# Two of eight one-hot comparisons per half chunk move from VectorE to GpSimd

## The reference, cut to what matters

```python
w = lut[idx]                               # lut: 16 numbers, idx: int32
return jnp.einsum('bsh,oh->bso', x, w)
```

## Time and profile before

| | |
|---|---|
| median of three runs | 1895.86 us (1895.57 to 1897.36) |
| profiled execution, span from first to last instruction | 1894.3 us |
| that execution's own device time | not given beside the span; the span is 1.6 us under the median |
| front block | from 0 to about 526 us of the span |
| VectorE busy, whole span | 1313.4 us (69%) |
| GpSimd busy, whole span | 791.7 us (42%) |
| mean granted TensorE clock | 0.890 |

### The profile page before, as it was taken

One profiled execution on the slowest core, in us unless ns is written; L12 is line 12 of the kernel. 1 busy time (PEld: TensorE's weight loads), 2 busy tenths in 40 slices (PEclk: granted clock), 3 DMA queues, 4 the chain that ended last, 5 costly groups with the idle time before them and its releaser, 6 DMA issues. The chain is left out here.

```text
span 1894.3 us, 26370 instructions
## 1 busy us (share of the span) xinstructions
PE 1535.1 (81%) x9320; PEld 1312.2 (69%) x9328; DVE 1313.4 (69%) x1918; ACT 910.7 (48%) x1579; POOL 791.7 (42%) x477
## 2 busy tenths in 40 slices
PE   5857778676528986996898799648899999999896
PEld 3445355444427986895897689637779899998785
DVE  6677597776559989999998999624445555555452
ACT  3444546445224445344444534414456666666563
POOL 1010000010045456445654643357735666762555
PEclk9879788897758997997998799858999999999998
DMA  7988799985572582375359236459998999999876
GB/s 210 344 282 273 280 323 369 332 266 176 165 311 77 191 345 76 124 278 223 106 190 372 73 119 236 165 189 342 388 365 235 253 260 259 256 261 220 228 168 78
DMA packets 187942, 445.47 MB, mean 235 GB/s; under 512 B 41616, under 2 KB 43664, under 8 KB 177568
## 3 DMA queue, kind: packets, MB, share of 16 engines
q1 hardware_dynamic: 115040, 283.37, 44.3%
q0 software_dynamic: 31760, 74.48, 16.8%
q10 hardware_dynamic: 41008, 85.89, 12.5%
HBM read 246.77 MB, written 205.28 MB: 239 GB/s over the span
## 5 line engine op out<-in xcount | busy, mean ns | idle before, releaser
L1429 POOL TENSOR_TENSOR mix_st<-mix_Bb,mix_du 128x2048 f32<-128x2048 f32 x64 | 293.4, 4584 | 267.9 <-DVE mix_st L2149 255.1
L2141 DVE TENSOR_TENSOR_SCAN mix_st<-mix_YY,mix_st 128x512 f32<-128x512 f32 x256 | 311.8, 1218 | 53.7 <-POOL mix_st L1429 32.2
L1847 ACT ACTIVATE mix_YY<-mix_dt,mix_A 128x512 f32<-128x512 f32 x256 | 176.9, 691 | 277.6 <-DVE mix_st L2141 273.6
L1473 POOL DMA_INDIRECT out_x<-moe_ys,moe_meta x130 | 209.6, 1613 | 192.4 <-ACT moe_ys L1973 93.5
L1594 PE MATMUL mix_G<-mix_xThi,mix_wup 128*128 128x256 f32 x1408 | 272.4, 290 | 15.2 <-issue 14.5
L1594 PEld LDWEIGHTS mix_G<-mix_xThi,mix_wup 128*128 128x128 f32 x1408 | 231.3, 199 | 18.1 <-issue 16.7
L1755 PE MATMUL mix_Dp<-moe_xhi,moe_whi 128*128 128x288 f32 x768 | 233.2, 304 | 1.1 <-DVE moe_wlo L2245 1.1
L1755 PE MATMUL mix_Dp<-moe_xhi,moe_wlo 128*128 128x288 f32 x768 | 227.5, 296 | 0.0
L1755 PE MATMUL mix_Dp<-moe_xlo,moe_whi 128*128 128x288 f32 x768 | 227.4, 296 | 0.0
L1620 PE MATMUL mix_YY<-mix_ident,mix_st 128*128 128x128 f32 x1024 | 145.2, 297 | 95.4 <-DVE mix_st L2149 95.2
L2255 DVE TENSOR_TENSOR moe_xlo<-mix_G,moe_xhi 128x512 fp32r<-128x512 f32 (+1 forms) x160 | 102.0, 638 | 163.1 <-ACT moe_xhi L1936 160.4
(11 more groups left out here) (216 smaller groups left out, 3059.5 us busy)
## 6 DMA issues: line engine op xcount, KB each, us to landing
x_by_expert<-front_zeros ACTq DMA_DIRECT2D x16, 4480.0 KB, 23.9
mix_wup<-w_halves SPq DMA_DIRECT2D x44, 1024.0 KB, 5.6
moe_raw<-in_ew SPq DMA_DIRECT2D x32, 1280.0 KB, 8.4
moe_xt<-x_by_expert SPq DMA_DIRECT2D x128, 256.0 KB, 8.4
mix_wdn<-w_halves SPq DMA_DIRECT2D x44, 512.0 KB, 6.5
front_idx<-in_idx SPq DMA_DIRECT2D x44, 384.0 KB, 9.1
w_halves<-front_wst SPq DMA_DIRECT2D x44, 384.0 KB, 7.8
mix_Bb<-bc_rows SPq DMA_DIRECT2D x16, 1024.0 KB, 9.9
```

Source lines behind the costliest of these rows:

```text
L1429: nc.gpsimd.tensor_tensor(st[:, g % STBUF, :, :], Bb[:, q, :, :], du[:, k % 2, :].unsqueeze(1).to_broadcast([P, NG, S]), ALU.mult).then_in ...
L1473: pool.indirect_dma_start(out=out_rows, out_offset=bass.IndirectOffsetOnAxis(ap=meta[0:rows, e % MBUF, j, 0:1].bitcast(U32), axis=0), in_= ...
L1847: nc.scalar.activation(dA, dt[:, k % 2, :], ACT.Exp, scale=A[:, c, m:m + 1]).then_inc(da_ready, 1)
L2141: nc.vector.tensor_tensor_scan(r, dA, r, 0.0, ALU.mult, ALU.add).then_inc(scanned, 1)
```

## The change

Of each half's eight one-hots GpSimd makes j = 2 and j = 6 and VectorE the other six. GpSimd runs the same comparison on the same operands, counted on a semaphore of its own; `lookup(t)` and `load_idx(h)` wait for whichever engine made the one-hot. `kcol` is signalled to GpSimd. GpSimd's one-hots stand in its list `AHEAD` = 4 slots ahead as well, the first two on either side of `scale_and_shift(0)`, and behind the other work of each slot.

```diff
+ON_POOL = (2, 6)
+def onehots(t, pool):
+    n = sum(1 for j in ON_POOL if j < t % PAIRS)
+    return len(ON_POOL) * (t // PAIRS) + n if pool else t - (len(ON_POOL) * (t // PAIRS) + n)
...
             def load_idx(h):
-                    sp.wait_ge(onehot_made, PAIRS * (h - 1))
+                    sp.wait_ge(onehot_made, onehots(PAIRS * (h - 1), False))
+                    sp.wait_ge(pool_onehot_made, onehots(PAIRS * (h - 1), True))
...
         def _(pool):
+            def one_hot(t):
+                h, j = divmod(t, PAIRS)
+                if t >= SLOTS or j not in ON_POOL:
+                    return
+                if j == ON_POOL[0]:
+                    pool.wait_ge(idx_in[h % 2], 32 * (h // 2) + 32)
+                if t >= OH:
+                    pool.wait_ge(slot_done, t - OH + 1)
+                nc.gpsimd.tensor_scalar(oh[:, t % OH, :], idx[:, h % 2, :], kcol[:, j:j + 1], None,
+                                        ALU.is_equal).then_inc(pool_onehot_made, 1)
+            pool.wait_ge(pool_kcol, 1)
+            for t in range(AHEAD - 2):
+                one_hot(t)
             scale_and_shift(0)
+            for t in range(AHEAD - 2, AHEAD):
+                one_hot(t)
             for t in range(SLOTS + 16):
...
+                one_hot(t + AHEAD)
...
             def lookup(t):
-                pe.wait_ge(onehot_made, t + 1)
+                if j in ON_POOL:
+                    pe.wait_ge(pool_onehot_made, onehots(t + 1, True))
+                else:
+                    pe.wait_ge(onehot_made, onehots(t + 1, False))
...
         def _(dve):
             def one_hot(t):
+                if j in ON_POOL:
+                    return
...
-            link(nc.vector.tensor_scalar(kcol[ROWS_H:P, :], kcol[ROWS_H:P, :], 1.0, None, ALU.add))
+            nc.vector.tensor_scalar(kcol[ROWS_H:P, :], kcol[ROWS_H:P, :], 1.0, None, ALU.add).then_inc(pool_kcol, 1)
+            dve.wait_ge(pool_kcol, 1)
```

More of the change, by code:

```diff
@@ L233, in front_block @@
         onehot_made = sem("onehot_made")
+        pool_onehot_made = sem("pool_onehot_made")
+        pool_kcol = sem("pool_kcol")
         slot_done = sem("slot_done")
```

## The result

The changed kernel takes 1945.66 us, median of four runs (1940.19 to 1947.55); the kernel before took 1895.71 beside it (1895.2 to 1897.36). The ratio is 1.0252, with a 95% interval of 1.0233 to 1.0271. That is 50 us slower, where 6 us faster was forecast, and it lies outside the range of 1878 to 1911. The profiled execution took 1945.0 us, of which the span is 1943.3.

The account below looks back on a forecast made before the run. Neither TensorE nor VectorE alone bounds the front block; VectorE sets the pace for part. Saving 10.2 less holds 4 gives 6.2 us: span 1894.3 to 1888.1, plus 1.6 for the median: 1889.7 us; range 1878 to 1911.

Parts of the forecast that it names:

- the price of GpSimd's comparison: One GpSimd one-hot of 1536 columns in the front block was taken at 1.5 us, with 3.4 as the other end.
- hold rival: GpSimd's comparison costs about 3.4 us and holds VectorE for more than is saved: 15 us slower, 1911 us; chance 0.30.
- What VectorE sheds: In the front block, 44 one-hots of 0.93 us leave VectorE, 40.9 us; 10.2 us was taken to reach the end.
- the 20.5 that was called a bound: At most one moved one-hot stands in each of TensorE's 22 waits for VectorE: 22 x 0.93 = 20.5 us.
- the half that was taken: Half of 20.5 us, so 10.2, since two of eight slots move and stretches of one-hots are one to five long.
- What they take from each other: In the front block GpSimd's one-hots hold VectorE; up to 1.3 us each, charged 1 us a batch, 4 in all.
- the laid-out places: GpSimd's one-hots laid on the third batch: slots 94 and 102 beside taps or reductions, slot 98 holding VectorE 0.5 us.
- Who is held: Only VectorE one-hots or instructions with two SBUF inputs would be held; PSUM reductions and taps would go on.
- Where GpSimd's time lies: 66 us of one-hots fit on GpSimd, busy 30 of 477; ready before their slots, without blocking its short tasks.
- turning point of 2.1 us: In the hold rival, the comparison time at which hold and saving are equal, with a quarter met.

Follow-up runs that it names:

- e15: Changed kernel with GpSimd's comparison replaced by a copy of the indices; only its front block counts: next block starts at 524.9 us, against 526.7 in the kernel before.
- e5: Kernel before, plus a row of GpSimd instruction forms run alone behind the last slot; only durations used: tensor_scalar on 1536 columns 4.1 to 4.2 us, converting copy 1.46.
- e1: Changed kernel with the 44 moved one-hots made by nobody; 1927.19 us against 1948.3 for the kernel before, ratio 0.9897.
- e2: Kernel before, with GpSimd making the 44 comparisons once more into a spare buffer nobody reads; 2015.2 us against 1948.3, ratio 1.0344.
- e3: Kernel before, with GpSimd running four powers of four columns at each of the 44 places; 1944.64 us against 1948.3, ratio 0.9975.
- e7: Changed kernel with each GpSimd comparison cut into two of 768 columns (halves); 1888.85 us against 1897.16 for the kernel before, ratio 0.9957.
- sixths: Changed kernel with each GpSimd comparison cut into six of 256 columns; 1897.22 us against 1897.16 for the kernel before, ratio 1.0003.
- thirds: Changed kernel with each GpSimd comparison cut into three of 512 columns; 1946.26 us against 1948.3 for the kernel before, ratio 0.9996.

## Why the prediction was wrong

**The step that failed is the price of GpSimd's comparison**: "I take 1.5 us and keep 3.4 as the other end". It measured 4.17 us, beyond both ends, and with a GpSimd instruction of 1.46 us in its place the stage is 54 us shorter (e15). The prediction chose by what the instruction does (reads one tensor, like a select), and ended its range at the arithmetic of two inputs, though it allowed that a form handled still more slowly can't be excluded. e5 shows that the form decides: a tensor_scalar costs 4.1 to 4.2 us for a comparison or a product, int32 or float32, and is dearer than two-input work. The length of GpSimd's instruction was the first thing that the prediction said to look at ("right at 1.3 to 2.1 us, wrong above"), and it was also the number on which its hold rival turned.

**What VectorE sheds.** In e1 VectorE is busy for 1271.6 us, 41.8 less than before (40.9 said). At the end it was worth 21.1, not the 10.2 that was taken, and more than the 20.5 that was called a bound. TensorE's waits for VectorE fell by 12.2 us, near the half that was taken. What the sum left out is the rest: 5.4 us that TensorE's matmuls got shorter at a higher granted clock, and some 2 us of other waits.

**TensorE's clock** has no term in the sum. It worked both ways: 5.4 us less of busy TensorE in e1, 15.7 more in the changed kernel, 22.9 more in e2 (371.8 us, at a granted clock of 0.79).

**What they take from each other.** The charge was 1 us a batch, 4 in all. With a 1.46 us instruction the holds rose by 17 us (e15), and of e1's 19.9 us of stage 1.8 were left: the charge should have been 18, over four times what was said. The saving was too small by two, and the two misses partly cancel; that is luck, not insight. At 4.17 us the holds rose by 100 us. A hold lasts up to 3.93 us, so 44 x 3.93 = 173 were possible, and 58% were met, against 17 of 44 x 1.3 = 57, or 30%, in e15. The share isn't a constant of the schedule, as the laid-out places took it to be. That an instruction of 4.2 us outlasts the reductions that it starts beside, and reaches what comes after them, would explain it; this is argued, not shown.

**Who is held.** "Only if VectorE's next instruction is a one-hot or has two SBUF inputs" missed the small tensor_scalar of the row scales: 26.9 of the 103 us, on the path to ScalarE's quantising. In e15 it missed `sc` (L877), the scales behind GpSimd's root: seven of its eight took 1.41 to 1.43 us in place of 0.17, 8.8 of the 17 us. Taps and reductions do go on, as said, and reciprocals too.

**Where GpSimd's time lies.** "It is ready long before its slot at 1.5 us, and at 3.4 too" held mostly: 8.5 us of waits for it at 4.3. That its order doesn't block the short tasks is borne out by e3. The block behind the barrier kept its length within 3 us, as said.

**The rival named hold** was right in mechanism. Its turning point of 2.1 us lies between what was run, about neutral at 1.46 and 50 us slower at 4.17, and is neither shown nor refuted. Its 1911 was too low, with 3.4 us for the price and a quarter for the share. In its own form, cost beside (e2) 66.9 less saving 21.1, it is 45.8.

**What stays open.** Why a comparison of 1536 columns holds VectorE to its end and one of up to 1024 only for under 1 ns a column, while it itself runs on; a copy of 1536 columns holds at most 1.27 us of its 1.46. The Trainium skill, SBUF — State Buffer, section Who interferes with whom, has the port pair locked for the whole instruction: the 3.73 us at 54.48 agree, the 0.82 us of e7 at 53.86 beside a 2.74 us instruction do not. It is also open why the best cut kernels bring 5 to 7 us of e1's 20. For halves, VectorE's busy time falls by 1313.4 - 1299.1 = 14.3 us net; at e1's rate, 19.9 / 41.8 = 0.48, that is 6.8 us, which fits. But the same sum gives 15 for sixths, where the stage is 0.8 shorter (with 31.5 us of waits for GpSimd), 10 for thirds, where it is 0.6 shorter, and a loss of 28 for the change, where it is 52.3. So VectorE's busy time doesn't tell the end.

## What to carry to other kernels

Before work moves to GpSimd, time the very form of instruction there, alone and at its full size: a neighbour that reads and writes as much can cost a third of it. Then ask not only whether it is ready in time, but what of VectorE's it holds while it runs, the smallest instructions too, and price that by how much it outlasts; a duplicate into a spare buffer measures it directly. If the move is still wanted, cut GpSimd's instruction into pieces: here two halves turned 50 us of loss into 6 to 8 of gain. A gain of that size, 0.3 to 0.4%, needs more than one series: here a kernel that spared nothing came out 3.7 us faster. And ask what TensorE's clock does when it waits more: here its own matmuls took 15.7 us more.

## What was not expected of the hardware

- GpSimd's tensor_scalar over 1536 columns takes 4.1 to 4.2 us, for the comparison and for the product; the copy takes 1.46, the memset 1.38, the two-input arithmetic 2.75. In pieces: 256 columns 0.92, 512 1.56, 768 2.2, 1024 2.75.
- It holds a VectorE instruction of two columns for up to 3.9 us, but not a reciprocal of the same size. VectorE goes on about 0.17 us before the recorded end of GpSimd's instruction.
- Powers of four columns on GpSimd hold nothing of VectorE's, at nearly 5 us in each place (e3).
- The length of a hold jumps between pieces of 1024 columns (0.89 us) and 1536 (3.93). A copy of 1536 holds for 1.27 at most.
